# Graph attention on one core: edge masks written once in float32 by ACT, and per-destination maxima as float32 products of nine columns

## The reference, cut to what matters

```python
h = (x @ W).reshape(N, HEADS, HEAD_DIM)          # 8 heads of 32
e = alpha_s[src] + alpha_d[dst]
e = jnp.where(e > 0, e, NEG_SLOPE * e)
m = jax.ops.segment_max(e, dst, num_segments=N)
ex = jnp.exp(e - m[dst])
denom = jax.ops.segment_sum(ex, dst, num_segments=N)
alpha = ex / (denom[dst] + 1e-16)
out = jax.ops.segment_sum(h[src] * alpha[:, :, None], dst, num_segments=N)
```

## Time and profile before

| quantity | us |
|---|---|
| time of a run, median of 3 | 2691.33 |
| lowest and highest | 2690.16, 2696.79 |
| span of the profiled execution | 2699.1 |
| busy in it: PE, PEld | 1965.3, 1549.3 |
| busy in it: DVE, POOL, ACT | 1600.0, 1408.9, 994.6 |
| gathers of convolution 0, first start to last | 1304.6 to 1821.4 |
| gathers of convolution 1 | 1916.9 to 2431.9 |

### The profile page before, as it was taken

How to read it: one execution, slowest core, us unless ns; L and a number is a source line. 1 busy time by engine, 2 the same in 40 slices (tenths; PEclk the granted TensorE clock), 3 DMA queues, 4 the chain that set the end, 5 groups by cost and what they waited for, 6 DMA issues and landing times.

```text
span 2699.1 us, 38166 instructions
## 1 busy us (share of the span) xinstructions
PE 1965.3 (73%) x10306; PEld 1549.3 (57%) x10306; DVE 1600.0 (59%) x5094; ACT 994.6 (37%) x2448; POOL 1408.9 (52%) x1415
## 2 busy tenths in 40 slices
PE   7999776676665799996366666675366666665799
PEld 5888644444445799995254454554345454454477
DVE  5200143434337655557378888888478888788744
ACT  4344200000001344443455555552545455452522
POOL 1100277777770234442577777770477777771233
PEclk9999877767775899998678788787778887787789
DMA  5544433333333899996444444440444444440000
GB/s 210 201 187 199 160 105 103 105 104 105 105 104 92 283 353 349 353 342 210 124 143 131 141 134 140 140 134 14 128 134 141 140 137 140 134 143 16 1 24 25
DMA packets 187265, 400.48 MB, mean 148 GB/s; under 512 B 30990, under 2 KB 98130, under 8 KB 180590
## 3 DMA queue, kind: packets, MB, share of 16 engines
q0 software_dynamic: 63520, 179.35, 23.4%
q1 hardware_dynamic: 112302, 187.97, 19.4%
q10 hardware_dynamic: 11232, 30.68, 3.4%
HBM read 323.15 MB, written 75.54 MB: 148 GB/s over the span
## 4 chain that ended last, share of the span: by engine, by line
PE 41%; POOL 23%; DVE 15%; issue 14%; DMA 3%; ACT 3%; DVEq 2%; ACTq 1%; POOLq 0%; SPq 0%
POOL arena L730 13%; POOL arena L1370 10%; PE banks L419 10%; PE banks L1165 9%; PE banks L1488 3%; PE banks L1177 3%; PE banks L1489 3%; DVE arena L1571 2%; DVE arena L1662 2%; PE banks L1459 2%; DMA arena<-ht,srcT 2%; PE banks L1329 1%; ACT arena L1413 1%; DVE arena L1627 1%; PE banks L2081 1%
## 5 line engine op out<-in xcount | busy, mean ns | idle before, releaser
L1370 POOL DMA_INDIRECT arena<-ht,srcT x784 | 793.4, 1012 | 310.8 <-issue 232.5
L730 POOL DMA_INDIRECT arena<-tr,idx1T x392 | 375.8, 959 | 327.0 <-DMA tr<-arena 207.9
L758 PE MATMUL banks<-arena 128*128 x884 | 339.0, 534 | 168.0 <-SPq L737 150.8
L1488 PE MATMUL banks<-arena,XT 128*128 128x264 f32 x884 | 372.3, 512 | 97.0 <-DVE arena L1662 73.2
L758 PEld LDWEIGHTS banks<-arena 128*128 128x128 f32 x884 | 214.3, 262 | 292.4 <-issue 259.6
L1489 PE MATMUL banks<-arena,XT 128*128 128x264 f32 x884 | 344.1, 479 | 0.0
L1662 DVE TENSOR_TENSOR arena<-arena,nrmT 128x528 f32<-128x528 f32 x448 | 312.9, 700 | 19.9 <-ACT nrmT L1435 19.9
L1488 PEld LDWEIGHTS banks<-arena,XT 128*128 128x128 f32 x884 | 211.9, 253 | 164.0 <-DVE arena L1662 83.5
L1413 ACT ACTIVATE arena<-iorow,dlT 128x128 bf16<-128x128 f32 x896 | 267.9, 387 | 65.4 <-issue 65.2
L419 PE MATMUL banks<-parts 128*128 128x512 f32 x1200 | 275.2, 391 | 4.7 <-DVE parts L379 4.7
L781 DVE TENSOR_TENSOR X<-X,banks 128x256 f32 x221 | 91.8, 415 | 312.6 <-PE banks L758 311.7
(11 more groups left out here) (363 smaller groups left out, 3156.7 us busy)
## 6 DMA issues: line engine op xcount, KB each, us to landing
arena<-in_L_ffn_w_dram SPq DMA_DIRECT2D x195, 512.0 KB, 6.0
tr<-arena SPq DMA_DIRECT2D x50, 1024.0 KB, 3.9
XT<-dld ACTq DMA_DIRECT2D x52, 512.0 KB, 4.4
arena<-ht,srcT POOLq DMA_INDIRECT x784
ht<-arena SPq DMA_DIRECT2D x50, 136.0 KB, 1.7
arena<-tr,idx1T POOLq DMA_INDIRECT x392
arena<-ys SPq DMA_DIRECT2D x8, 640.0 KB, 5.9
arena<-in_L_gnn_weight_dram SPq DMA_DIRECT2D x8, 512.0 KB, 9.0
```

The costliest lines, as they stand in the source:

```text
L730: pool.indirect_dma_start(Gr[:, o:o + D], None, TR, bass.IndirectOffsetOnAxis(ap=idx1T[:, q:q + 1], axis=0)).then_inc(d_g[b % NG], 16)
L758: mm = ten.matmul(B[n][:, 0:D], OHr[:, n, h, :], Gr[:, h * D:][:, bass.ds(o, D)], start=(h == 0), stop=(h == 1))
L1370: pool.indirect_dma_start(Gall[:, o:o + ROW], None, HT[L], bass.IndirectOffsetOnAxis(ap=srcT[:, q:q + 1], axis=0)).then_inc(d_g[b % NG], 16)
L1488: ten.matmul(B[n][:, 0:MSG], OH[b][:, 2 * j, :], WG[:, j, 0, :], start=True, stop=False)
```

## The change

Three things change, all inside the two convolutions.

1. `masks` writes float32 into one of **three** buffers `OH` (the turned masks `OT` move out of `XT` to make room); `widen`, its semaphore and the bfloat16 buffers go. A buffer is written again when the products of the chunk three before are done.
2. `ends` writes the product of the maxima and the flags straight into `SM`, nine columns of float32 a half; the call of `thirds` for it goes. `across` copies the flag as float32.
3. `maxima` multiplies float32 masks with float32 `SM`: 9 columns a half in place of 25. `values` has one addition from PSUM where it had a copy and three additions.

```diff
@@ act_gat
             def masks(c):
-                b, k = c % 2, L * NCH + c
-                if c > 1:
-                    act.wait_ge(oh_ok, k - 1)
-                    act.wait_ge(mx_ok, k - 1)
+                b = c % 3
+                if c > 2:
+                    act.wait_ge(pr_ok, 2 * (L * NCH + c - 2))
                 for j in range(CC):
                     q = c * CC + j
-                    v = ac.put(act.activation(OHb[b][:, j, :], iorow[:, :], ACT.Abs, scale=-1.0, bias=dlT[:, q:q + 1]))
+                    v = ac.put(act.activation(OH[b][:, j, :], iorow[:, :], ACT.Abs, scale=-1.0, bias=dlT[:, q:q + 1]))
                 act.wait_ge(ac.sem, v)
-                act.activation(OHb[b], OHb[b], ACT.Relu, scale=-1.0, bias=onec[:, 0:1]).then_inc(ob_ok, 1)
-
-            def widen(c):
-                b, k = c % 2, L * NCH + c
-                act.wait_ge(ob_ok, k + 1)
-                if c > 1:
-                    act.wait_ge(pr_ok, 2 * (L * NCH + c - 1))
-                act.copy(OH[b], OHb[b]).then_inc(oh_ok, 1)
+                act.activation(OH[b], OH[b], ACT.Relu, scale=-1.0, bias=onec[:, 0:1]).then_inc(ob_ok, 1)
...
-                    widen(n)
@@ pe_gat
                 ten.wait_ge(ob_ok, k + 1)
-                ten.wait_ge(sb_ok, k + 1)
+                ten.wait_ge(sm_ok, k + 1)
                 if c:
                     ten.wait_ge(vv_ok, k)
                 for j in range(CC):
-                    n = 25 * (j // 2)
-                    mm = ten.matmul(B[6][:, n:n + 25], OHb[b][:, j, :], SB[:, j, 0:25], start=(j % 2 == 0), stop=(j % 2 == 1))
+                    n = 9 * (j // 2)
+                    mm = ten.matmul(B[6][:, n:n + 9], OH[b][:, j, :], SM[:, j, :], start=(j % 2 == 0), stop=(j % 2 == 1))
@@ dve_gat, ends
-                vec.wait_ge(sm_ok, k + 1)
-                yield from thirds(lambda t: SB[:, :, (0, 9, 17)[t]:(8, 17, 25)[t]], SM, SM, sb_ok, 0)
@@ dve_gat, values
-                u = dv.put(vec.tensor_copy(VV, pm[:, :, 17:25]))
-                yield
-                for t in (9, 0):
-                    vec.wait_ge(dv.sem, u)
-                    u = dv.put(vec.tensor_tensor(VV, VV, pm[:, :, t:t + 8], ALU.add))
-                    yield
-                vec.wait_ge(dv.sem, u)
-                vec.tensor_tensor(VV, VV, vp.rearrange("p (s o) -> p s o", o=1).to_broadcast([P, CH, 8]),
+                vec.wait_ge(dv.sem, v)
+                vec.tensor_tensor(VV, pm[:, :, 0:8], vp.rearrange("p (s o) -> p s o", o=1).to_broadcast([P, CH, 8]),
                                   ALU.add).then_inc(vv_ok, 1)
```

More of the change, by code:

```diff
@@ L1263, in build @@
         AS, SC = [xn[:, 0, i * P:(i + 1) * P] for i in range(2)], xn[0:8 * CH, 1, :]
-        SM, EE, VV = (v.rearrange("p (s c) -> p s c", c=8) for v in (xn[:, 2, 0:P], xn[:, 3, 0:P], nrmT[:, 0:8 * CH]))
+        EE, VV = (v.rearrange("p (s c) -> p s c", c=8) for v in (xn[:, 3, 0:P], nrmT[:, 0:8 * CH]))
         EX = [nrmT[:, (1 + i) * P:(2 + i) * P].rearrange("p (s c) -> p s c", c=8) for i in range(2)]
@@ L1281, in build @@
         xtf = XT[:, :, :].rearrange("p k n -> p (k n)")
-        OH = [xtf[:, i * CC * P:(i + 1) * CC * P].rearrange("p (s c) -> p s c", c=P) for i in range(2)]
-        OT = [xtf[:, (4 + i) * CC * P // 2:(5 + i) * CC * P // 2].bitcast(BF16) for i in range(2)]
+        OH = [xtf[:, i * CC * P:(i + 1) * CC * P].rearrange("p (s c) -> p s c", c=P) for i in range(3)]
         hst = Gall[:, 24 * 2 * ROW:26 * 2 * ROW].rearrange("p (b c) -> p b c", b=4)
-        SB = take(CC * 13, dt=BF16).rearrange("p (s c) -> p s c", c=26)
-        OHb = [take(CC * P // 2, dt=BF16).rearrange("p (s c) -> p s c", c=P) for _ in range(2)]
+        SM = take(CC * 9).rearrange("p (s c) -> p s c", c=9)
+        OT = [take(CC * P // 2, dt=BF16) for _ in range(2)]
         vp = take(CH)
@@ L1303, in build @@
         pm_ok, p2_ok, pj_ok, one_ok = (sem(n) for n in ("pm_ok", "p2_ok", "pj_ok", "one_ok"))
[L1304 to L1307, removed]
+        as_ok, spread_ok, scan_ok, back_ok, sm_ok, mx_ok, vv_ok, sp_ok, ee_ok, x_in, x_ok = (sem(n) for n in (
+            "as_ok", "spread_ok", "scan_ok", "back_ok", "sm_ok", "mx_ok", "vv_ok", "sp_ok", "ee_ok", "x_in", "x_ok"))
+        w_ok, f_in, f_ok, pr_ok, ad_ok, ob_ok, ot_ok = (sem(n) for n in (
+            "w_ok", "f_in", "f_ok", "pr_ok", "ad_ok", "ob_ok", "ot_ok"))
         sc_ok = sem("sc_ok")
@@ L1463, in maxima @@
             def maxima(c):
-                b, k = c % 2, L * NCH + c
+                b, k = c % 3, L * NCH + c
                 ten.wait_ge(scan_ok, k + 1)
@@ L1586, in ends @@
                 vec.wait_ge(back_ok, k + 1)
-                vec.tensor_tensor(SM.rearrange("p (s a) h -> p s a h", a=2),
+                vec.tensor_tensor(SM[:, :, 0:8].rearrange("p (s a) h -> p s a h", a=2),
                                   B[7][:, EW:EW + P].rearrange("p (a s h) -> p s a h", a=2, h=8),
@@ L1600, in across @@
                 la = laT[:, c * CC:(c + 1) * CC].rearrange("p (s o) -> p s o", o=1)
-                dv.put(vec.tensor_copy(SB[:, :, 8:9], la))
+                dv.put(vec.tensor_copy(SM[:, :, 8:9], la))
                 yield
@@ L1605, in values @@
                 k = L * NCH + c
-                pm = B[6][:, 0:25 * CH].rearrange("p (s c) -> p s c", c=25)
+                pm = B[6][:, 0:9 * CH].rearrange("p (s c) -> p s c", c=9)
                 mo_.load(c * CH)
```

2 lines of the change are left out of this document (removed).

## The result

| | before | after |
|---|---|---|
| median of a run, us | 2692.16 (4 runs, 2690.16 to 2696.79) | 2746.07 (4 runs, 2738.68 to 2757.14) |
| ratio | | 1.020, 95% interval 1.017 to 1.023 |
| span of the profiled execution | 2699.1 | 2738.1 |

The change costs 54 us, 2%. The forecast was +3 us and its range ended at 2720, so both missed; "slower" had been given 0.30. In every ratio of this document, executions over 1.5% longer than the fastest of the same kernel are left out.

A forecast was written before the change was run, and what follows sets the result against it. Bound by POOL's gathers (18.7 us a chunk) and the loop's turn (18.50), 1% apart. Late products 0.53 minus DVE's gain 0.30 is 0.23 a turn, 12 us over 54 turns; a quarter lands: +3 us, median 2694, range 2680 to 2720.

The forecast's parts named there:

- The price of a record: Maxima on PE: a narrow float32 record costs 0.110 us at full clock, so 32 cost 3.52, bounds 0.55 to 7.04.
- The start: Maxima on PE start once `SM` is written, 0.67 us after `expand` in place of 2.58.
- DVE before the Exp: DVE's chain from `expand` to the Exp loses five instructions: 2.68 us for 2.98, gain 0.30 a turn.
- ACT and POOL: Removing `widen` (1.88 us) gains nothing, ACT's wait before the Exp becomes about 7 us; POOL's gathers stay unchanged.
- The threshold M = 4.98: M, the maxima's end after `expand`, 4.35 us at full clock; past 4.98 the next turn's second-half product is late.
- x, the cold time behind `expand`: Time added to the maxima by a dropped clock, 2 x 3.43 x (1 - clock) us; a product is late above 0.63.
- 9 are late, by 11 us together: 0.53 us a turn: Of 21 sampled turns, 9 have maxima ending too late for the next turn's product, costing 0.53 us a turn.
- The rival's loop: In the slower rival, one late turn leaves PE idle between transposes and products, making the next colder: 0.9 us lost a turn.
- the quarter that was to land: Of 12 us over 54 turns only a quarter, +3 us, shows, since the gathers' pace covers the mean turn.
- the turns grow past the gathers: Slower rival: convolution turns exceed the gathers' pace, 0.9 us lost a turn, 2718 us; chance 0.30.
- The float32 maxima keep the clock up: Faster rival: the clock never drops, the maxima always end at 4.35 us, no product late, -8 us, 2683; chance 0.09.
- the gathers get shorter: Faster rival: fewer DVE instructions shorten POOL's gathers by 0.7 us a chunk, 16 us off, 2675; chance 0.05.

The follow-up runs named there:

- e10: Kernel with float32 masks but the three bfloat16 maxima parts kept, plus 32 unread narrow float32 records behind products 0 to 3: 1.0209 of the kernel before.
- e8: Changed kernel with six unread float32 products of 256 columns put ahead of the maxima: 1.0381 of the kernel before on the same chip.
- e9: Changed kernel with the second eight maxima products moved behind products 0 to 3 and `values` eight places later: 1.0360 of the kernel before.
- e1: Kernel before with ACT's float32 masks in three buffers, copied to bfloat16 for the old maxima, ring 23 blocks for 25; chip A: 1.0016 of the kernel before.
- e5: Kernel before with ACT's float32 masks in three buffers, copied to bfloat16 for the old maxima, ring 23 blocks for 25; chip B: 1.0023 of the kernel before.
- e11: Kernel before with ACT's float32 masks in three buffers, copied to bfloat16 for the old maxima, ring 23 blocks for 25; chip D: 1.0016 of the kernel before.

## Why the prediction was wrong

- **The price of a record: right.** 0.110 at the full clock gave 3.52 for 32; the shortest set took 3.71 on the first chip and 3.63 in e10. Twice that was the bound for a cold PE; 6.97 is what the records show.
- **The start: right.** The maxima start 0.69 after `expand` (0.67 predicted).
- **DVE before the Exp: right.** From 1616 to the Exp 2.65 (1526.98 - 1524.33); 2.68 predicted, 2.98 before.
- **ACT and POOL: right.** ACT waits 175.9 / 27 = 6.5 before the Exp (7 predicted). The gathers' median is 953 ns (956 before) and their mean 1013 (1012), so the shorter DVE chain did not speed them up.
- **The threshold M = 4.98: right.** With the gain of 0.30 and the 0.2 that the gathers forgive, a turn should grow once M passes 5.48, that is a length above 4.75; in the table the intervals are 18.62 up to 4.7 and grow from there.
- **What failed: x, the cold time behind `expand`, and with it "9 are late, by 11 us together: 0.53 us a turn".** I read the granted clock in the trace of before, in 21 turns, mean x 0.84, M 5.19 (redone, the 9 late turns give 10.8 us and 0.51 a turn). In the changed kernel M, taken from where DVE starts `values`, is 6.22 on average and 47 of 50 turns are late, by 1.26 in the mean. 1.26 - 0.30 = 0.96; of that the gathers' slack covers some 0.2, which leaves 0.76 a turn, and 0.82 was measured. The sum's form holds; one term was less than half of its size.
- **Why x was wrong.** Not the choice of turns: all 50 steady turns of before, treated alike, give x 0.71 and M 5.06. The same reading in the trace of the changed kernel gives x 1.84. The clock does not stay as it was when the work on it changes. Over 52 turns it fell 3.6 us after `expand` before and 2.3 after, and stayed at 0.50 for 5.1 us before and 8.3 after. e8, e9 and e10 show that what stands right ahead sets the clock of such records. What makes it fall sooner on the first chip stays open. The rival's loop (a late turn makes the next colder) is not borne out: a long M does lengthen the next turn, counted between the transposes of the scores (correlation 0.71 over 48 pairs), but the length of one set goes with that of the next set by 0.2 only. Its reason, an idle PE between transposes and products, explains it only in part, since PE stands less in the changed kernel and not more (442 us busy for 324.5).
- **What failed with it: "A turn is then about 18.6 to 18.7, still at the pace of the gathers", and the quarter that was to land.** With 0.96 a turn against 0.2 of slack most of it lands, and POOL waits 34.4 us for room over both convolutions (2.4 before).
- **The rivals.** The true one was "the turns grow past the gathers": it was to decide once the loss net of the gain passed 0.5, and that was 0.96; it was priced at 0.9 of loss before the gain, where 1.26 came, though its loop is not shown. "The float32 maxima keep the clock up" is refuted by the 0.50 of the shown turn; "the gathers get shorter" by the mean of 1013.

The Trainium skill, "Perfetto Trace Analysis", Matmul Optimizations, says that the matmul engine scales its power with utilization, so that products should run back to back. e10 agrees (3.63 us behind products back to back, 6.97 behind an idle PE, for the same records). On the first chip the busy share alone misleads: it rose from 63% to 85% of convolution 0 and the clock fell from 0.79 to 0.76.

## What to carry to other kernels

A float32 record of few columns is not cheaper than one of many: 0.113 us with 9 columns (3.63 / 32) and 0.117 with 128, both at the full clock, with the weight load busy for 309.5 of the 313.2 us of the maxima. So going from three narrow bfloat16 parts to one float32 product (32 records of 0.11 to 0.22 us for 16 that took 0.55 together) pays for DVE's and ACT's saved time with PE's; do it only where PE has room for the longer of the two. Price work that is moved onto a chain at both clocks, and take the half clock unless wide products stand right ahead of it: a clock that is read from the trace of before belongs to the work of before. Where two limits lie within 1% of each other, a loss on the covered one shows, less that 1%, as soon as it is larger.

## What the runs showed of the hardware

**Narrow bfloat16 products cost the same at both clocks.** 16 of 25 columns took 0.55 at 0.96 and 0.58 at 0.50 (e1, e5, e11), 0.034 and 0.036 each; 32 float32 ones of 9 columns took 3.63 and 6.97. float32r ones cost as float32 (0.22 each at 0.50). The Trainium skill, "TensorE: Matmul & The Clock Gate", Weight-path perf modes, has a fast weight load for 128 weights of types other than FP32, and no win for fp32. The rows agree for bfloat16 and float32, and float32r's 0.22 gives no sign of it here.

**A stall that the first chip does not have.** On chips A to E DVE stands for a semaphore that PE should have given long before, while POOL gathers. In the first gather stage of e1:

```profile
637.18 0.96 POOL L730 DMA_INDIRECT arena<-tr,idx1T  x1 [0.30 <-issue]
642.03 0.42 DVE L781 TENSOR_TENSOR X<-X,banks 128x256 f32 x1 [23.24 <-remote]
642.27 0.95 POOL L730 DMA_INDIRECT arena<-tr,idx1T  x1 [4.13 <-remote]
...
643.18 2.07 PE L758 MATMUL banks<-arena 128*128 x4 [16.78 <-DVE arena L772]
```

DVE and POOL wait for the same products of PE, whose last record begins 16 us earlier, and both go on at 642.0 to 642.3, 4.9 us after the start of the last gather. This repeats every 34 us through that stage, 389.9 us in 17 waits, up to 42.0. (On the first chip 781 waits for these products too, 311.7 us in 55 waits, but 15.0 at most, and POOL does not stand with it.) In the convolutions the first instruction of the weights (1638) does the same, 378.7 us in 45 waits, up to 14.3 each. It starts up to 11.8 us after `expand` has ended, 5.1 on average; in the last turns of a convolution, with no gather left, it starts 0.04 after it, as in every turn of before on the first chip. In e10, where PE's queue differs, the stall moved to the scan, another reader of a product of PE. Neither kernel has such a wait in its trace of the first chip. By the Trainium skill, "Perfetto Trace Analysis", Tensor Engine Instruction, a record's end on this engine is estimated, and the semaphore is given when PSUM has acknowledged the write; so the records can't tell a late product from a late semaphore. No run tried to settle the cause, and it stays open. It goes with some 190 us more in each convolution's loop on A (732 and 733 in e1, 542 in the kernel before on the first) and some 100 more in the first gather stage (one wait of ACT across it is 607.5 us in e1 and 511.8 in the kernel before), which is why the 54 us could not be measured piece by piece on one like the first.
